# A second buffer for the turned rows of x, two turns in the loop's body, and one transposing step for both sets of row factors

## The reference

```python
# layer 1, 8 heads of 128: cosine attention without softmax, mixed from three parts
f_q, f_k, f_v = proj(layer_norm(x)), proj(ctx), proj(ctx)
cosine_sim = dots / (qn[..., None] * kn[..., None, :])
var_component = q_ratio[..., None] * k_ratio[..., None, :]
mixed = cw * cosine_sim + vw * cosine_sim * decorr_scale + ww * var_component
x = x + tanh(g_xattn) * (mixed @ f_v @ w_out.T + b_out)
# layer 2, 16 heads of 16: softmax over the queries of each key, two row normalisations, gelu
z = layer_norm(x); scores = k @ q.T / 16; attn = softmax(scores, -1)
z = l2n(l2n((attn.T @ v) @ Wo) @ Wff)
x = x + tanh(g_ffn) * gelu(z)
```

## Time and profile before

| | |
|---|---|
| median of 3 runs | 1333.44 us (1329.61 to 1336.89) |
| the profiled execution: its time, its span | 1331.52 us, 1329.8 us |
| busy: TensorE, VectorE, ScalarE, GpSimd | 1197.1 (90%), 1116.6 (84%), 1012.5 (76%), 206.9 (16%) us |
| transfers | 162.3 MB, mean 122 GB/s |

### The profile page before, as it was taken

How to read it: one execution, slowest core, us unless ns; L and a number is a source line. 1 busy time by engine, 2 the same in 40 slices (tenths; PEclk the granted TensorE clock), 3 DMA queues, 4 the chain that set the end, 5 groups by cost and what they waited for, 6 DMA issues and landing times. The chain is left out here.

```text
span 1329.8 us, 34850 instructions
## 1 busy us (share of the span) xinstructions
PE 1197.1 (90%) x10386; PEld 744.4 (56%) x10386; DVE 1116.6 (84%) x3180; ACT 1012.5 (76%) x3333; POOL 206.9 (16%) x160
## 2 busy tenths in 40 slices
PE   4999967999999999999989899989898999898965
PEld 2677536565646464656565656565555656564531
DVE  5986546798989898989898898989898989898964
ACT  5667113487979797979797979797888888888887
POOL 1443101202020202011110202020202020202000
PEclk9999879999999999999999999999999999999987
DMA  8450024463627281818181818182727254544650
GB/s 257 136 166 20 3 53 80 132 124 111 158 92 176 74 194 50 218 47 220 45 204 51 204 52 208 42 213 52 200 68 194 74 182 85 170 98 142 112 159 17
DMA packets 247888, 162.30 MB, mean 122 GB/s; under 512 B 94538, under 2 KB 235559, under 8 KB 247848
## 3 DMA queue, kind: packets, MB, share of 16 engines
q1 hardware_dynamic: 247848, 161.80, 46.3%
HBM read 86.74 MB, written 42.58 MB: 97 GB/s over the span
## 5 line engine op out<-in xcount | busy, mean ns | idle before, releaser
L1529 ACT ACTIVATE prob<-score,nm 128x256 f32<-128x256 f32 x1024 | 474.9, 485 | 61.4 <-DVE nm L1722 34.0
L1722 DVE TENSOR_REDUCE nm<-score 128x2 f32<-128x512 f32 x512 | 337.3, 681 | 17.2 <-PE score L1433 16.0
L1529 ACT ACTIVATION_READ_ACCUMULATOR prob<-score,nm 128x1 f32 x1024 | 222.5, 217 | 0.0
L1444 PE MATMUL attended<-prob,vsp 128*32 128x256 f32 x2048 | 134.9, 392 | 8.5 <-DVE vsp L1737 7.6
L1433 PE MATMUL score<-qstack,kstack 64*128 64x256 f16 x1024 | 97.0, 277 | 38.6 <-DMA kstack<-parts 27.4
L1642 DVE BATCH_NORM_STATS2 qst<-work 128x6 f32<-128x128 f32 x512 | 112.0, 284 | 22.3 <-PE work L895 22.3
L1588 POOL TENSOR_TENSOR l2r<-l2v,mhalf 128x4 f32<-128x4 f32 x16 | 16.1, 1009 | 599.0 <-DVE l2v L1694 599.0
L893 PE MATMUL work<-wTh,xTh 128*128 128x512 f16 x256 | 98.3, 384 | 5.4 <-DVE xTl L1636 3.5
L894 PE MATMUL work<-wTl,xTh 128*128 128x512 f16 x256 | 98.0, 383 | 0.0
L895 PE MATMUL work<-wTh,xTl 128*128 128x512 f16 x256 | 97.8, 382 | 0.0
L893 PE MATMUL work<-Vph,mTh 128*128 128x256 f16 (+1 forms) x320 | 87.4, 273 | 5.7 <-issue 4.8
...
## 6 DMA issues: line engine op xcount, KB each, us to landing
qstack<-parts SPq DMA_DIRECT2D x64, 256.0 KB, 3.8
kstack<-parts SPq DMA_DIRECT2D x64, 256.0 KB, 4.3
...
parts<-qh SPq DMA_DIRECT2D x32, 256.0 KB, 2.5
parts<-ql SPq DMA_DIRECT2D x32, 256.0 KB, 2.7
```

What stands on the lines that cost most here:

```text
L1444: last = nc.tensor.matmul(pvb[32 * j:32 * j + 32, t, :], vsp[:, k, (4 * e + j) * 2 * FD:(4 * e + j + 1) * 2 * FD], prob[:, n % PG, e, j, : ...
L1529: nc.scalar.activation(prob[:, g % PG, e, j + jj, :], sc[n % SC][:, jj * NQ:(jj + 1) * NQ], ACT.Exp, bias=nm[:, u + jj:u + jj + 1], accum_ ...
L1722: nc.vector.tensor_reduce(nm[:, u:u + 2], sc[n % SC][:, :].rearrange("p (u q) -> p u q", q=NQ), AX.X, ALU.max, negate=True).then_inc(max_r ...
```

## The change

Three things change, and with them the order.

- `xT` becomes a list of two pairs; the pair of batches a uses buffer a modulo 2 (`turned`). The second one takes its place from `kr`, a tile of the setup phase, and ScalarE waits once for the stores of `kr`. The loop's body now holds two turns, and the loop runs 7 times.
- `aux` becomes one tile of columns, eight for the first set of factors and eight for the second, 32 columns apart, in four groups. `a0` transposes both sets at once, with 128 columns of `aux` for each of the four row tiles; the first set lands in rows 0 to 7 of the bank, the second in rows 32 to 39. `a1` is gone. `a0.v` copies the first, `a0.h` and `a0.l` the second; `wqT` lies in rows 32 to 39 of `sqT`'s tile. GpSimd clears `aux` once at the start.
- `ORDER`, `HEAD`, `TAIL` and `MOVED` are new. 46 chunks are left in a turn. Low halves are on VectorE before and after.

The diff, with HEAD and TAIL left out:

```diff
 ORDER = """
-G0 X1 G1.h M2 G2.l G0.h qs2 G3 G3.h ldx S2 M3 G1.l G0.l G3.l a0 X2 a0.v res V3 V5 pv1 V3.h M4 V5.h aux back1 M5 V3.l
-V0 X3 rk X4 V5.l z back2 pv1.v R0 S3 V4 V0.h fk0 V4.h X5 P0 M6 S4 X6 M7 V0.l V4.l fk0.h X7 sqe0 V2 M8 sqe1 fk0.l M9
-V2.h fk1 V2.l R1 X8 X9 S5 fk1.h vt1 a1 d0 M10 M11 X10 fk1.l vt0 S6 M12 a1.h P1 a1.l fk2 X11 d0.o E0 S7 fk2.h m0.h M13
-d1 L0 d2 R2 P2 X12 fk2.l M14 m0.l M15 X13 X14 d3 X15 d1.o d2.o S8 m1.h M16 d4 R3 m2.h M17 S9 m1.l X16 m2.l d3.o wq ldy
-d5 X17 d4.o P3 E1 S10 zT0 M18 m3.h zT0.h m4.h M19 y0 X18 m3.l m4.l X19 d5.o m5.h M20 zT1 zT0.f zT1.h L1 m5.l M21 zT0.l
-S11 y0.o M22 y1 X20 zT1.f M23 R4 zT1.l y1.o X21 X22 ln1 O0 X23 R5 back3 O1 q0 S12 S13 P4 O0. P5 lpow q0.o M24 M25 M26
-O1. M27 q1 q2 ln2 q1.o q3 X24 q2.o q3.o zz0 X25 X26 X27 S14 S15 M28 zz1 zz0.h zz0.l E2 zz1.h q4 X28 M29 q5 zz1.l q4.o
-M30 pk0 X29 X30 q6 q5.o M31 X31 pq0 pk0.h L2 R6 pq0.h R7 pk0.l P6 q6.o P7 q7 pq0.l E3 L3 O2 q7.o O2. O3 G5 qs1 pq1 O3.
-G5.h G5.l F1 F2 parts0 pq1.h V1 V1.h back0 pk1 S0 pq1.l G4 V1.l F3 M0 pk1.h pk1.l G4.h G4.l G1 M1 parts1 X0 F4 pv0
-pv0.v qpow G2 S1 G2.h out
+qs2 V0 ldx V1.h V1.l X1 G1 V0.h M3 V0.l G1.h a0 S2 a0.v G5 a0.h G1.l pv1 rk G5.h X2 aux M4 X3 G5.l pv1.v a0.l V2 M5 V4
+V2.h z S3 back1 V4.h G0 X4 V2.l R0 M6 V4.l G2 P0 G0.h G4 G0.l X5 sqe0 M7 G2.h S4 G2.l V5 M8 fk0 X6 X7 R1 G4.h M9 G4.l
+S5 X8 fk0.h M10 V5.h P1 M11 d0 X9 E0 X10 sqe1 V5.l fk0.l d0.o S6 L0 M12 zT0 X11 zT0.h fk2 R2 m0.h M13 zT0.f fk2.h m0.l
+d1 S7 X12 P2 X13 fk2.l wq M14 d2 X14 M15 X15 d1.o d2.o fk1 vt1 zT0.l m1.h S8 fk1.h M16 zT1 R3 M17 vt0 zT1.h d3 fk1.l
+S9 zT1.f m1.l zT1.l M18 P3 m2.h X16 d3.o res X17 M19 m2.l d4 q0 d4.o X18 q1 S10 X19 q0.o m3.h E1 back3 m3.l S11 d5 M20
+m4.h d5.o m5.h m4.l m5.l X20 q1.o M21 L1 M22 y0 ldy X21 y1 X22 M23 X23 R4 S12 y0.o R5 y1.o M24 M25 S13 ln1 P4 P5 X24
+M26 O0 X25 lpow O1 O0. O1. M27 X26 q2 q3 X27 ln2 zz0 q2.o S14 q3.o M28 S15 zz0.h zz1 zz1.h X28 q4 zz0.l zz1.l q5 E2
+M29 X29 pk0 M30 q4.o M31 q5.o L2 X30 pq0 X31 R6 q6 R7 pk0.h P6 pq0.h P7 pq0.l pk0.l E3 q6.o L3 q7 O2 parts0 O3 O2.
+q7.o O3. pq1 back0 V3 pk1 F1 V3.h qs1 S0 S1 V3.l back2 pq1.h pq1.l F2 pk1.h G3 pk1.l qpow F3 M0 V1 pv0 M1 parts1 X0
+G3.h M2 F4 pv0.v out G3.l
 """.split()
...
-MOVED = {step: n for n, steps in {0: "G1 G2 G2.h G4 G4.h G4.l G5 G5.h G5.l V1 V1.h V1.l qpow qs1", 1: "M0 M1 S0 S1 X0", 2: "back1 back2 back3 pv1 pv1.v res"}.items() for step in steps.split()}
+MOVED = {step: n for n, steps in {0: "G3 G3.h G3.l V1 V3 V3.h V3.l qpow qs1", 1: "M0 M1 M2 S0 S1 X0", 2: "back1 back3 pv1 pv1.v res"}.items() for step in steps.split()}
...
-    xT, mT, zzT, oT = pair("xT", [P, KT, PR]), pair("mT", [P, 2, HT, 2 * P]), pair("zzT", [P, KT, PR]), pair("oT", [P, 2, PR])
+    xT, mT, zzT, oT = [pair("xT", [P, KT, PR]), w["xT1"]], pair("mT", [P, 2, HT, 2 * P]), pair("zzT", [P, KT, PR]), pair("oT", [P, 2, PR])
...
-    aux, sqT, wqT = sb("aux", [P, 2, PT, H]), sb("sqT", [H, PR]), pair("wqT", [H, PR])
+    aux, sqT, wqT = sb("aux", [P, (PT - 1) * (AUX + H) + P]), sb("sqT", [AUX + H, PR]), {}
...
+    both = sqT[AUX:AUX + H, :].bitcast(F16)
+    wqT["h"], wqT["l"] = both[:, 0:PR], both[:, PR:2 * PR]
+
+    aux_cols = aux[:, 0:PT * (AUX + H)].rearrange("p (t c) -> p t c", c=AUX + H)
...
+    looped = {"odd": 0}
+
+    def turned(pair):
+
+        return xT[pair % 2 if isinstance(pair, int) else looped["odd"]]
...
-        with eng.Fori(0, NPAIR - 2) as i:
-            for s in ORDER:
-                part_of(s, i + 2 - lead(s))
+        with eng.Fori(0, (NPAIR - 2) // 2) as i:
+            for odd in range(2):
+                for s in ORDER:
+                    looped["odd"] = (odd + lead(s)) % 2
+                    part_of(s, i * 2 + odd + 2 - lead(s))
...
-                    pe.wait_ge((sq_ready, wqr_ready)[c], a + 1)
+                    pe.wait_ge(sq_ready, a + 1)
+                    pe.wait_ge(wqr_ready, a + 1)
                     for t in range(PT):
-                        last = nc.tensor.transpose(bk[0:H, t * P:(t + 1) * P], aux[:, c, t, :], ident[:])
+                        last = nc.tensor.transpose(bk[:, t * P:(t + 1) * P], aux[:, t * (AUX + H):t * (AUX + H) + P], ident[:])
...
+                        if isinstance(a, int) and a == 1:
+                            act.wait_ge(w["kr_stored"], 64)
...
-                    drain(nc.scalar.activation(sqT[:], bank(e)[0:H, :], ACT.Copy), e)
-                elif e == "a1" and part == "h":
+                    nc.scalar.activation(sqT[0:H, :], bank(e)[0:H, :], ACT.Copy).then_inc(sqT_ready, 1)
+                elif e == "a0" and part == "h":
                     wait_filled(act, a, e)
                     act.wait_ge(wq_in, a * 32)
-                    nc.scalar.activation(wqT["h"][:], bank(e)[0:H, :], ACT.Copy, scale=MS).then_inc(hi_ready[lead("a1.h")], 1)
+                    nc.scalar.activation(wqT["h"], bank(e)[AUX:AUX + H, :], ACT.Copy,
+                                         scale=MS).then_inc(hi_ready[lead("a0.h")], 1)
...
-                elif e == "a1" and part == "l":
+                elif e == "a0" and part == "l":
+                    dve.wait_ge(sqT_ready, a + 1)
                     dve.wait_ge(*halved(e, a))
-                    drain(nc.vector.scalar_tensor_tensor(wqT["l"][:], bank(e)[0:H, :], MS, wqT["h"][:],
-                                                         ALU.mult, ALU.subtract), e)
+                    drain(nc.vector.scalar_tensor_tensor(wqT["l"], bank(e)[AUX:AUX + H, :], MS,
+                                                         wqT["h"], ALU.mult, ALU.subtract), e)
```

More of the change, by code:

```diff
@@ L970 @@
-+q1.o +lpow +q2 +ln2 +q3 +zz0 +zz0.h +q2.o +q3.o +zz0.l +zz1 +q4 +zz1.h +zz1.l +q5 +q4.o +pk0 +q5.o +pq0 +pk0.h +pq0.h
-+q6 +pk0.l +pq0.l +q6.o +q7 +q7.o +pq1 +pq1.h +parts0 +G5 +back0 +pq1.l +G5.h +G4 +V1 +V1.h +G5.l +qs1 +qpow +G4.h
-+pk1 +G4.l +G2 +pk1.h +S0 +V1.l +G2.h +pk1.l +pv0 +M0 +X0 +parts1 +S1 +M1 +G1 +pv0.v
+fk0 ldx fk0.h fk0.l fk2 z zT0 fk2.h zT0.h zT0.f fk2.l zT1 zT1.h zT0.l zT1.f fk1 zT1.l fk1.h fk1.l q0 q1 q0.o q1.o q2
+q3 q2.o q3.o q4 q5 q4.o V3 q5.o q6 V3.h V3.l q6.o q7 q7.o V1 qs1 +V0 G3 G3.h +V1.h +ldy G3.l +ldx +V1.l qpow +G1 +qs2
@@ new lines @@
++V0.h +V0.l +a0 +G1.h +z +a0.v +a0.h +G5 +a0.l +aux +G5.h +V2 +G5.l +wq +V4 +V2.h +V4.h +G1.l +rk +sqe0 +V4.l +V2.l
++G0 +G4 +G2 +G0.h +G0.l +G2.h +G4.h +V5 +G2.l +V5.h +V5.l +fk0 +G4.l +zT0 +d0 +fk0.h +zT0.h +fk0.l +sqe1 +d0.o +fk2
++d1 +m0.h +zT0.f +m0.l +fk2.h +fk2.l +d1.o +d2 +fk1 +fk1.h +vt1 +d2.o +zT0.l +fk1.l +zT1 +m1.h +zT1.h +d3 +zT1.f +d4
++m1.l +m2.h +zT1.l +d3.o +q0 +m3.h +m2.l +d4.o +q0.o +q1 +m3.l +d5 +vt0 +d5.o +m4.h +q1.o +m4.l +y0 +m5.h +m5.l +y1
++y0.o +y1.o +q2 +ln1 +q3 +lpow +q2.o +ln2 +q3.o +zz0 +zz0.h +zz0.l +zz1 +q4 +zz1.h +zz1.l +q5 +q4.o +pk0 +q5.o +pq0
@@ L973 @@
++pk0.h +pq0.h +q6 +pk0.l +pq0.l +q7 +q6.o +q7.o +V3 +parts0 +qs1 +pq1 +pq1.h +pk1 +pk1.h +V3.h +pq1.l +G3 +qpow +pk1.l
++pv0 +back0 +V3.l +G3.h +G3.l +V1 +S0 +pv0.v +M0 +parts1 +back2 +X0 +M1 +S1 +M2
 """.split()
 TAIL = """
-qs2 G2.l G0 G1.h back2 X1 G0.h G3 G3.h G1.l M2 M3 a0 a0.v S2 G0.l V3 G3.l V5 pv1 M4 X2 X3 V3.h V3.l aux M5 V5.h X4 V0
-V5.l S3 pv1.v V4 V0.h back1 R0 rk M6 V0.l res X5 S4 M7 V4.h X6 X7 P0 V4.l V2 sqe0 a1 V2.h M8 M9 X8 V2.l R1 S5 d0 sqe1
-X9 M10 M11 X10 a1.h d0.o S6 P1 M12 a1.l vt1 X11 M13 X12 R2 S7 d1 vt0 m0.h E0 M14 wq X13 L0 d2 P2 M15 d1.o m0.l d2.o
@@ L978 @@
-X14 X15 S8 d3 m1.h d4 R3 m2.h M16 m1.l m2.l M17 d5 ldy X16 back3 X17 S9 P3 d3.o d4.o m3.h m4.h E1 M18 m3.l d5.o S10
-X18 M19 m5.h m4.l X19 y0 S11 m5.l L1 y0.o y1 R4 M20 M21 O0 X20 X21 M22 O1 M23 y1.o S12 ln1 X22 X23 lpow M24 O0. P4 O1.
-X24 M25 X25 S13 M26 S14 ln2 X26 M27 zz0 R5 zz1 M28 P5 M29 X27 zz0.h zz1.h zz0.l X28 S15 zz1.l pk0 M30 R6 pq0 M31 X29
-X30 E2 X31 pk0.h L2 R7 pq0.h P6 pk0.l pq0.l P7 E3 L3 O2 parts0 O2. O3 back0 O3. pq1 pk1 pq1.h pq1.l F1 pk1.h F2 S0 F3
-pk1.l M0 M1 S1 pv0 F4 X0 parts1 pv0.v out +pv1 +M2 +X1 +M3 +S2 +X2 +back1 +M4 +X3 +pv1.v +X4 +S3 +M5 +res +X5 +R0 +M6
@@ L983 @@
[L983 to L986 removed]
+V1.h V0 qs2 G1 X1 V0.h V1.l a0 G1.h V0.l a0.v a0.h G1.l S2 X2 M3 a0.l back1 pv1 G5 M4 X3 aux pv1.v V2 G5.h res M5 G5.l
@@ new lines @@
+E2 pk0 L2 X29 P6 X30 X31 R7 pk0.h pq0.h P7 E3 pk0.l pq0.l parts0 L3 O2 O3 back0 O2. O3. pq1 pq1.h pk1 F1 pq1.l F2 S0
+pk1.h pk1.l M0 pv0 S1 M1 F3 M2 F4 X0 pv0.v +M3 +X1 +X2 +pv1 parts1 +X3 +S2 +pv1.v +M4 +M5 back2 +R0 +S3 +M6 +M7 +X4
++X5 +X6 +back1 +X7 out +S4 +M8 +P0 +M9 +S5 +R1 +X8 +X9 +S6 +M10 +X10 +P1 +M11 +M12 +X11 +M13 +X12 +S7 +E0 +M14 +X13
++L0 +S8 +R2 +X14 +M15 +X15 +M16 +P2 +M17 +X16 +X17 +S9 +M18 +X18 +R3 +M19 +S10 +M20 +M21 +X19 +R4 +P3 +S11 +back3 +M22
++E1 +L1 +M23 +X20 +X21 +res +S12 +X22 +P4 +X23 +M24 +X24 +S13 +M25 +M26 +X25 +O0 +X26 +R5 +S14 +P5 +M27 +X27 +S15 +E2
@@ L1354, in a_part @@
                     for k in range(KT):
-                        last = products(nc, bk[:, :], xT, (ALL, k, slice(t * P, (t + 1) * P)),
+                        last = products(nc, bk[:, :], turned(a), (ALL, k, slice(t * P, (t + 1) * P)),
```

(3 more changed lines are left out.)

52 lines of the change are left out of this document (27 added, 25 removed).

## The result

The changed kernel takes **1361.3 us** (median of 4 runs, 1357.5 to 1365.2) beside 1332.9 for the kernel before on the same chip: a ratio of 1.021, 95% interval 1.017 to 1.026. It is slower by 2.1%; forecast were 1335 us and a range of 1311 to 1356. The profiled execution took 1365.2 us, 1.7 more than its span.

A forecast was written before the change was run, and what follows sets the result against it. No engine alone was taken as the bound, but how three fixed-order queues hand work on. From 1331.5 us: -3.5 for turns, +6 for branches, -1 for head and tail, 1333.0 (+1.5); forecast 1335 us, range 1311 to 1356.

The forecast's parts named there:

- part 4: Two turns in the loop's body: instruction fetches at 6 backward branches cost 0 to 18 us, 6 taken.
- Rival (b): Backward branches: the doubled body is fetched anew at each, 6 x 2.5 = 15 us, 1345 us; chance 0.19.
- (c): Turn's edge: TensorE's deficit stays whole, 69.8 us a turn, 15 us in all, 1349 us; chance 0.14.
- Part 1: Row factors in one step: the four transposes of a1 go, -0.55 us of TensorE's time a turn.
- Part 2: Second buffer of turned x: removes no work, only idle time, gaining between 0 and 2.2 us a turn.
- The slack behind P0: TensorE's idle time from P0 to the end of O3: 2.2 us a turn, 49.7 passing against 47.5 of products.
- Rival (a): Whole turn: the freer order pays, 67.5 us a turn with fetches hidden, 1317 us; chance 0.31.
- Part 3: New order at the turn's edge, walked through from rows: a turn takes 67.2 to 69.8 us, 68.45 taken.
- V0's wait for v: Turn's edge on TensorE: V0 waits 2 to 3 us a turn for v.
- The wait of st for x: VectorE's wait for x from memory, 1.02 us a turn, goes; by itself this frees nothing on TensorE.
- Head and tail: Before and after the loop: -1 us, between -4 and +2; the tail has the same work.
- The signs I had named: Marks to check in the trace: turn length, waits, transposes, idle time, and over 80 instruction packets if fetched each time.

The follow-up runs named there:

- e2: The changed kernel with its loop written out, 14 turns in a row without a branch: 1335.6 us, 1.001 times the kernel before.
- e15: The changed kernel with the loop of two turns on TensorE alone, every other engine's written out: 1340.7 us, 1.011 times the kernel before.
- e8: The kernel before, with its order, one buffer and one turn in the body, and only a0 and a1 merged: 1352.7 us, 1.014 times the kernel before.
- e13: The changed kernel with its loop written out, run again in a later batch: 1336.8 us, 1.006 times the kernel before.
- e14: The written-out changed kernel with unread products on TensorE where it waits at the turn's edge, second run: 1331.1 us, 1.002 times the kernel before.

## Why the prediction was wrong, step by step

**The step that failed is part 4, the body of two turns,** in its size and in what it left out. It said 1 us for each of 6 branches, 18 us as the ceiling, and gave the branch anew-fetched 0.19. Measured are 25.7 us for the branches (changed kernel against its written-out self, 4.3 each). In place of a body that mostly fits or is fetched ahead, ScalarE's and VectorE's bodies were fetched anew at every branch: 90 instruction packets on their queue in the loop, where it had none. Three things were wrong. First, residence was left open with the odds on "it fits", though nothing in the trace showed more than one turn's 1305 instructions of TensorE going round. Second, the price was taken from a store's landing, 2.5 to 2.9 us, and then cut to 1 us on the ground that sequencers run ahead; none did here over a branch to a body that was gone: "issue" is 19.8 / 6 = 3.3 us a branch on VectorE and 16.3 / 6 = 2.7 on ScalarE. Third, TensorE's clock was no term at all. It was 1.00 in the loop, and I took it as given; at each branch it is 0.50 for 6.8 us or more. How much of the 4.3 us is the clock I can't separate. The stall at a0 is 14.0 / 6 = 2.3. The changed kernel has 58.0 - 23.9 = 34.1 us more at 0.50 than e2, in which TensorE can lose at most half, 17 us or 2.8 a branch, an estimate from these rows; that the clock is the rest is likely and not shown.

The reason for 1 us that named TensorE was right: "TensorE's idle time at the edge covers its own share" is what e15 measured, 0.65 us a branch. The half about ScalarE and VectorE, "critical just there", was the case. Rival (b) was this mechanism, at 2.5 us a branch and 1345 us; its sum with 4.3 would have been 1333.4 - 3.5 + 26 = 1356. The range, too, took only a third of part 4's own ceiling with (c); with the whole of it it would have reached 1349 + 18 = 1367 and held the result.

The Trainium skill, "Runtime: NRT & Kernel Launch", section "Instruction fetch mechanics", gives sizes (2048 instructions for TensorE, 512 for most others) with which this case agrees: bodies of 1305 (TensorE) and 298 (VectorE) stay, of 2587, 595 and 587 (ScalarE) don't. No body nearer to the limits was run. By them rival (b) had to be the forecast. I let its other statement, of a window of two blocks, which the earlier trace rows contradict, count against the sizes too.

**Part 1.** The four transposes went (TensorE has 64 matmuls fewer). Alone the merged step is no gain but a loss (e8, +18 us), where the rotation of the banks moves with it and a0's bank is held longer. That TensorE would wait for VectorE's low half of a0 had no term; it is 4.0 us in 7 waits in the changed kernel.

**Part 2.** The slack behind P0 did come out. From P0 to the end of O3 TensorE had gaps of 1.1 us in most turns of the kernel before, in 49.9 us; in e2 it has none at all, in 50.1, with more products in the stretch. By the prediction's own pricing, 48.9 us of products, 1.2 of the 2.2 us of slack are left, near the middle between its bounds. Rival (a) put half of this slack at 0.65 us, where half of 2.2 is 1.1; with that its time would have been 67.1 a turn.

**Part 3, the walk along the edge.** It said 67.2 to 69.8 us and took 68.45; the written-out kernel has 68.44 in its undisturbed turns, which is nearer than a middle of two bounds deserves: luck. The mean over e2's turns is 69.0. V0's wait for v was to be 2 to 3 us: 34.8 / 14 = 2.5. The wait of st for x was to go: it has no row any more (14.3 us). But I priced V0's wait at 1.2 us of deficit alone; its other price, 0.4 us a turn through the clock (e13 and e14), I did not see. Forecast for the 14 turns were -3.5 us; with the clock's falls e13's loop is 964.7 against 961.9 in the kernel before, +2.8, across two batches.

**Head and tail.** The head was to gain 1 us and gained 1.7 (262.9 against 264.6 us up to the first mark). The tail, taken as equal, lost 3.3: 106.6 us from the loop's end against 103.3. In sum: -1.7 + 32.1 + 3.3 = 33.7, the difference of the spans.

**The signs I had named** told it at once: over 80 packets on the first instruction queue, and turns that begin with a branch longer than those between. That is (b), and (c), alike turns, is excluded.
